# Grouping the narrow and wide matmul forms of a two-stage convolution, and storing the last two images in 8 KB pieces

## What is computed

```python
def _L0_conv_ref(x, w3, b3, w5, b5, wr, br):
    y3 = conv(x, w3, 'SAME') + b3
    y5 = conv(x, w5, 'SAME') + b5
    P = pad(y3, 1)
    shifts = [P[:, :, 2 - sw:2 - sw + H, 2 - sh:2 - sh + W] for sh in range(3) for sw in range(3)]
    stacked = stack([y5] + shifts, axis=2)
    return einsum('bcghw,cg->bchw', stacked, wr) + br

def _L1_conv_ref(x, filters):            # 3 x 3 patches, a leading 1, and all products of two entries
    spot = concatenate([ones, patches(x, 3)], -1)          # 10 numbers
    feat = spot[..., :, None] * spot[..., None, :]         # 100 products
    return einsum('bcyxf,ocf->boyx', feat, filters)

x = x + _L0_conv_ref(_gn(x), ...)
x = x + _L1_conv_ref(_gn(x), filters)
```

## Time and profile before

| | |
|---|---|
| median of 3 runs | 304.58 us |
| profiled execution, its own time | 305.6 us |
| its span | 303.9 us |
| mean granted TensorE clock | 0.979 |
| PE busy | 276.0 us (91%), 6464 records |
| DVE busy | 251.5 us (83%) |
| ACT busy | 88.1 us (29%) |
| DMA | 11.45 MB, of it 4.19 MB written |

### The profile page before, as it was taken

The page is one execution under the profiler, slowest core; times in us unless marked ns, Lnnn a source line. Parts: engine busy times, 40 slices in busy tenths (PEclk is TensorE's granted clock), DMA queues, the critical chain, the costliest instruction groups (busy, mean ns, idle before and its releaser), DMA issues.

```text
span 303.9 us, 13566 instructions
## 1 busy us (share of the span) xinstructions
PE 276.0 (91%) x6464; PEld 125.6 (41%) x6464; DVE 251.5 (83%) x216; ACT 88.1 (29%) x135; POOL 33.0 (11%) x82
## 2 busy tenths in 40 slices
PE   0579999899999999999999999999999999999930
PEld 0124443343334434436457455333334446447310
DVE  1899899995999999599999999976999999950330
ACT  5432016949258989529000000004000000000000
POOL 7913970000110000000000000000000000000000
PEclk9999999979999999999999999999999999999985
DMA  6973000000000000000000000085000000000049
GB/s 191 382 193 82 4 3 2 2 5 2 2 2 4 4 2 2 4 2 5 2 2 4 4 2 4 2 172 111 2 2 4 2 2 4 2 4 4 2 86 190
DMA packets 19206, 11.45 MB, mean 38 GB/s; under 512 B 17744, under 2 KB 17872, under 8 KB 19024
## 3 DMA queue, kind: packets, MB, share of 16 engines
q1 hardware_dynamic: 14640, 9.06, 11.7%
q10 hardware_dynamic: 4512, 1.53, 2.2%
HBM read 6.40 MB, written 4.19 MB: 35 GB/s over the span
## 4 chain that ended last, share of the span: by engine, by line
PE 80%; DVE 7%; ACT 3%; issue 3%; DMA 2%; SPq 1%; DVEq 0%
PE acc L1007 63%; PE acc L1050 15%; ACT raw L507 3%; DMA raw<-in_x 2%; DVE stats L741 2%; PE acc L1101 2%; DVE plane L759 1%; DVE raw L801 1%; DVE arena L669 1%; ACT arena L497 1%; DVE scaled L637 0%; DVE norm L756 0%; SPq L314 0%; SPq L321 0%; DVE mean_var L746 0%
## 5 line engine op out<-in xcount | busy, mean ns | idle before, releaser
L1007 PE MATMUL acc<-product,weight 32*32 32x512 f32 (+1 forms) x3040 | 128.6, 605 | 0.0
L1007 PEld LDWEIGHTS acc<-product,weight 32*32 32x32 f32 (+1 forms) x3040 | 61.7, 110 | 63.8 <-issue 51.1
L879 DVE TENSOR_TENSOR product<-plane 128x4096 f32<-128x4096 f32 x19 | 83.3, 4427 | 0.1
L1007 PE MATMUL acc<-raw,weight 32*32 32x512 f32 (+1 forms) x992 | 44.3, 605 | 0.0
L1050 PE MATMUL acc<-product,middle 32*64 32x512 f32 (+1 forms) x576 | 30.6, 621 | 0.0
L1007 PEld LDWEIGHTS acc<-raw,weight 32*32 32x32 f32 (+1 forms) x992 | 20.4, 111 | 20.7 <-issue 16.2
L801 DVE TENSOR_TENSOR raw<-acc,arena 128x512 f32<-128x512 f32 x16 | 9.9, 684 | 18.9 <-issue 18.7
L741 DVE BATCH_NORM_STATS2 stats<-raw 128x6 f32<-128x512 f32 x32 | 19.7, 686 | 3.1 <-DMA raw<-in_x 3.1
L879 DVE TENSOR_TENSOR raw<-plane 128x4096 f32<-128x4096 f32 x5 | 22.2, 4433 | 0.0
L1007 PE MATMUL acc<-product,arena 32*32 32x512 f32 (+1 forms) x448 | 22.0, 606 | 0.0
L507 ACT ACTIVATE raw<-arena 32x512 f32<-32x512 f32 x32 | 21.9, 683 | 0.5
(11 more groups left out here) (121 smaller groups left out, 213.9 us busy)
## 6 DMA issues: line engine op xcount, KB each, us to landing
raw<-in_x SPq DMA_DIRECT2D x8, 512.0 KB, 8.5
out<-raw SPq DMA_DIRECT2D x24, 128.0 KB, 2.9
arena<-in_L_conv_filters SPq DMA_DIRECT2D x4, 400.0 KB, 6.9
out<-raw ACTq DMA_DIRECT2D x8, 128.0 KB, 4.6
arena<-in_L_conv_w ACTq DMA_DIRECT2D x4, 100.0 KB, 4.0
w_in<-in_L_conv_w ACTq DMA_DIRECT2D x2, 36.0 KB, 1.9
w_in<-in_L_conv_w SPq DMA_DIRECT2D x2, 36.0 KB, 2.1
b_in<-in_L_conv_b SPq DMA_DIRECT2D x2, 0.5 KB
```

The lines of the kernel that those rows point to most:

```text
L879: nc.vector.tensor_tensor(both_halves(g, u), plane_halves(g), plane_halves(g, PRODUCTS[k][0] * PITCH + PRODUCTS[k][1]), ALU.mult)\
L1007: return nc.tensor.matmul(acc[32 * s:32 * (s + strips), j, r, :], weights[32 * r:32 * r + 32, t:t + strips, :] .rearrange("p t c -> p (t c ...
```

## The change

It has five parts.

1. In the second layer's mixed and side units the forms of several units are grouped: all pairs of linear, square and next one after another, then all singles, where before each unit had its own pair and single part. `mixed_unit` and `side_unit` now issue one form per call.
2. In `PRODUCTS` the entries (2, -1) and (1, -2) change places. The first is all singles, so that now (2, -1) and (2, 0) follow one another (units 15 and 16).
3. In the first layer of group 1 the border correction stands elsewhere: between its two parts there are 16 pairs of the block "total" instead of 16 singles, and the rest of that block starts with singles. In the second layer of group 0 the first 32 singles come ahead of the border's first part and the 32 pairs between its parts, where it was the other way round.
4. The last eviction (`evict_last`): images 0 and 1 as before. Images 2 and 3 are evicted strip by strip, 32 partitions x 512 elements each, straight into image layout on partitions 64 to 95 and 96 to 127 of `product[2]`.
5. Their store: SyncE and ScalarE's queue each send one half of the image rows of each of the two images, 256 KB, from 32 partitions, in runs of 8 KB. The small stores of images 0 and 1 stay.

```diff
-PRODUCTS = ((0, 0), (0, 1), (1, 1), (1, -1), (0, 2), (2, 2), (2, -2), (2, 1), (1, 2), (2, -1), (1, -2), (2, 0), (1, 0))
+PRODUCTS = ((0, 0), (0, 1), (1, 1), (1, -1), (0, 2), (2, 2), (2, -2), (2, 1), (1, 2), (1, -2), (2, -1), (2, 0), (1, 0))
...
+        def whole_image(r):
+            return product[2][32 * r:32 * r + 32, 0:PIX].rearrange("p (y x) -> p y x", x=W)
+
+        def store_last(eng, strips):
+            before = 2 * GROUP + 2 + 2 * STRIPS
+            for r in (0, 1):
+                eng.wait_ge(evicted, before + r + 1)
+                store(eng, 1, r, strips)
+            side = strips[0] // 2
+            for r in (2, 3):
+                eng.wait_ge(evicted, before + 2 + STRIPS * (r - 2) + 2 * side + 2)
+                eng.dma_start(out[GROUP + r][:, SIDE_ROWS * side:SIDE_ROWS * (side + 1), :],
+                              whole_image(r)[:, SIDE_ROWS * side:SIDE_ROWS * (side + 1), :]).then_inc(stored, 16)
...
+            def evict_last(odd):
...
+                for r in (0, 1):
+                    nc.vector.tensor_tensor(view(result, 2 * CHUNK * r + odd, (W, CHUNK // HALF_W), (2, HALF_W)),
...
+                for r in (2, 3):
+                    for s in range(STRIPS):
+                        y = SIDE_ROWS * (s // 2) + 1 - s % 2
+                        nc.vector.tensor_tensor(whole_image(r)[:, y:y + SIDE_ROWS - 1:2, odd:odd + W - 1:2],
+                                                acc[32 * s:32 * s + 32, odd, r, :]
...
+                                                ALU.add).then_inc(evicted, 1)
...
             product0(1, "next", 0, False, False, False)
             edges0(0, ROW_SIDES)
-            product0(1, "total", 0, False, False, False)
+            product0(1, "total", 0, False, False, True, (-1, 0))
             edges0(0, COLUMN_SIDES)
-            product0(1, "total", 0, False, True, True).then_inc(part_done, 1)
+            product0(1, "total", 0, False, False, True, (1, 2))
+            product0(1, "total", 0, False, True, False).then_inc(part_done, 1)
             pe.wait_ge(edges_copied, 2)
-            rest0(1, PAIRS_FIRST)
+            rest0(1, SINGLES_FIRST)
```

More of the change, by code:

```diff
@@ L604, in _ @@
             keep_cross(1)
-            for r in range(GROUP):
-                act.wait_ge(evicted, 3 * GROUP + r + 1)
-                store(act, 1, r, (2, 3))
+            store_last(act, (2, 3))
         @block.vector
@@ L1042, in plane_pixels, with column0 @@
                 return pixels
-            def column0(odd, stack, at, pitch, x0, every, five, start, stop, pairs):
+            def column0(odd, stack, at, pitch, x0, every, five, start, stop, pairs, rows):
                 def tile(r, s, strips, d, t, first_one, last_one):
@@ L1054, in column0 @@
                 if pairs:
[L1055 removed]
+                    for d in rows:
                         for s in (0, 2):
@@ L1064, in column0, with product0 @@
                 return last
-            def product0(g, name, odd, start, stop, pairs):
+            def product0(g, name, odd, start, stop, pairs, rows=range(-1, 3)):
                 if name == "next":
@@ L1070, in product0 @@
                     return column0(odd, plane[g], PLANE_AT - 2 * PITCH, PITCH, 2, 2, weight0[:, PAIR_AT:EDGE_AT, :],
-                                   start, stop, pairs)
+                                   start, stop, pairs, rows)
                 source, x0 = ("step", 1) if name == "step after" else (name, 0)
@@ L1077, in product0 @@
                 pe.wait_ge(middle_ready, g + 1)
-                return column0(odd, *half_at(g, source), x0, 1, five, start, stop, pairs)
+                return column0(odd, *half_at(g, source), x0, 1, five, start, stop, pairs, rows)
             def part(g, names, odd, forms):
@@ L1169, in mixed_unit, with side_unit @@
                     taps = (cross_taps if j else sum_taps)[0][:, 3:6, :]
-                for pairs in forms:
-                    last = column(j, stream_pixels(g, UNIT_OF[name][0], j), every_row, taps,
-                                  start and pairs == forms[0], stop and pairs == forms[-1], pairs)
-                return last
-            def side_unit(g, j, name, forms, start=False):
+                return column(j, stream_pixels(g, UNIT_OF[name][0], j), every_row, taps, start, stop, pairs)
+            def side_unit(g, j, name, pairs, start=False):
                 pe.wait_ge(stream_made, made(g, name + (" right" if j else " left")))
@@ L1181, in side_unit @@
                     a = {"linear": 0, "square": 9}[name] + 6 * j
-                for pairs in forms:
-                    last = column(j, stream_pixels(g, UNIT_OF[name][1], j), every_row, weight1[:, a:a + 3, :],
-                                  start and pairs == forms[0], False, pairs)
-                return last
+                return column(j, stream_pixels(g, UNIT_OF[name][1], j), every_row, weight1[:, a:a + 3, :],
+                              start, False, pairs)
             def taps1(g, j, u, pairs, stop=False):
```

96 lines of the change are left out of this document (62 added, 34 removed).

## The result

The changed kernel takes 303.59 us, the median of nine runs (302.55 to 304.27), beside 304.66 for nine runs of the kernel before. The ratio is 0.9945 (95% interval 0.9923 to 0.9967). The medians are 1.1 us apart, the ratio says 1.7 (1.0 to 2.3); 3.3 were forecast. The forecast of 301.3 was 2.3 us too low, though the time is inside its range. The profiled execution took 303.59 us too, with a span of 301.9.

A forecast was written before the change was run, and what follows sets the result against it. TensorE's pace and a store tail of some 10 us were taken as the bound. Runs -2.4, waits 0, first border -0.5, tail -0.1 and second border -0.3 made -3.3, from 304.58 to 301.3 us; range 298.4 to 303.9.

The forecast's parts named there:

- ten evictions 0.60 us apart: VectorE's last evictions: ten per half take 6.0 us, so half 1 starts at most 0.1 us late.
- The tail's rate: Final stores: large pieces from 32 partitions go at the filter load's rate, 219 GB/s at full share.
- The gain of 0.2: Final stores: 1 MB of large pieces takes 4.8 us against 5.0, with 0.1 us lost to the late start.
- the slower rival: Final stores: large pieces starve each other at half the filter's rate, tail 4.6 us longer, 306.0 us; chance 0.08.
- The rival at 408 GB/s: Final stores: large pieces run at the image load's rate, 2.3 us more off the tail, 299.0 us; chance 0.15.
- The runs of one form: TensorE behind 101 us: seven fewer changes from singles to pairs at 0.34 us each, 2.4 us less.
- the waits: TensorE, second layer: some 0.5 us more for square left, evened by the 0.6 us border-copy wait going; sum 0.
- The second border: Second layer's border correction, where 32 pairs now cover its start: estimated at 0.3 us less.
- The first border: First layer's border correction: stop shrinks from 1.8 to about 0.9 us, step done 0.35 us sooner; 0.5 us less in all.
- The clock: TensorE behind the first border: rival that the fall to 1.2 GHz goes too, worth 1.5 to 1.7 us, 299.7 us; chance 0.25.
- long waits for product streams: TensorE: rival that grouping turns into waits for streams, or the stop does not move, 303.7 us; chance 0.12.

The follow-up runs named there:

- e1: The changed kernel with the last evictions and stores of the kernel before: 302.1 us, ratio 0.9925 to the kernel before.
- e2: The kernel before with only the small evictions of images 2 and 3 and their stores in 8 KB runs: 305.9 us, ratio 1.0036.
- e7: The changed kernel with images 1 and 3 as the large stores, SyncE's queue sending all of image 1, ScalarE's all of image 3: 302.15 us, ratio 0.9903.
- e8: The changed kernel with the old tail and, in group 0, the singles of next ahead of those of square left: 302.71 us, ratio 0.993.
- e4: The kernel before with grouped forms, exchanged products and the second border's new order, but the old first border and tail: 303.41 us, ratio 0.9956.
- e5: The changed kernel with images 2 and 3 evicted in 32-partition pieces that stay in place, stored as before in small runs: 303.67 us, ratio 0.9968.

## Why the prediction was right in direction and wrong in size

**The failed step: ten evictions 0.60 us apart.** The prediction wrote that 32 partitions cost the same, that "ten take 10 x 0.60 = 6.0 us", and that half 1 starts at most 0.1 us late. The length was right (0.69 us either way), the distance was not. The overlap of 0.09 us that the large ones have was taken for granted, and it is lost wherever the starting partition changes: 2 x 0.60 + 0.12 + 8 x 0.72 = 7.1 us, and half 1 is 1.13 us late. Since half 1's stores are the tail, all of that is in the time: e1 against the changed kernel 1.1 us in the trace, e2 against before 1.1 us in the median. The number that was multiplied by ten came from the earlier trace rows, from evictions over 128 partitions; no row of before showed another shape at this place. The late start was put at 0.1 us and is 1.13; this alone takes 1.0 us of the 3.3 that were forecast. A bound was to be had: the page of before gives that line a mean length of 684 ns, so without overlap ten take 2 x 0.60 + 8 x 0.69 = 6.7 us at least.

**The tail's rate was as forecast.** The large pieces go at what the small ones did, 209 GB/s, and the tail stays 12.5 us. It had been taken from the filter load, 219 at full share, because the pieces are read from few partitions, and e7 supports that reason. The gain of 0.2 didn't come; the slower rival's half rate didn't either. The rival at 408 GB/s could not come in this form, with both queues on one half; e7 shows that 1.4 us of it were to be had.

**The runs of one form, -2.4, and the waits, 0.** The cost of a change was well sized: from the first pairs behind the second border (102.06 us before, 100.63 after) to half 0's first eviction there are 183.40 us before and 181.65 after, 1.75 less, and 2.35 without the wait that follows. One place stands out. Weight loads of the changed kernel, twice a run of 96 singles and the pairs behind it:

```profile
106.09 0.29 PEld L1039 LDWEIGHTS acc<-product,arena 32*32 32x32 f32 x32 [0.81 <-DVE product L911]
...
109.90 0.24 PEld L1039 LDWEIGHTS acc<-product,weight 32*32 32x32 f32 x32 [1.24 <-DVE product L904]
...
113.33 0.23 PEld L1039 LDWEIGHTS acc<-raw,weight 32*64 32x64 f32 x16 [0.89 <-issue]
...
143.69 0.29 PEld L1039 LDWEIGHTS acc<-product,weight 32*32 32x32 f32 x32 [0.85 <-issue]
...
150.33 0.23 PEld L1039 LDWEIGHTS acc<-raw,weight 32*64 32x64 f32 x16 [0.88 <-issue]
```

The first run takes 113.33 - 106.09 = 7.24 us, the second 150.33 - 143.69 = 6.64: 0.60 us are the wait for "square left". The prediction had named it, at 0.5, and set against it the wait for ScalarE's border copy, 0.6. That one did not go: it is 0.5 still. So the term of the waits is +0.5, not 0: the second step that failed. The prediction set one wait off against another that it only supposed to end. (e8 shows that without it TensorE would meet most of it again further down.)

**The second border, -0.3.** TensorE's timeline from the second layer's start to the first mixed single behind its border, first of the kernel before, then of the changed one:

```profile
91.44 4.01 PE L1007 MATMUL acc<-plane,arena 32*64 32x512 f32 x64 [0.69 <-DVE arena L669]
...
100.65 0.67 PE L1007 MATMUL acc<-product,arena 32*32 32x512 f32 x6
```

```profile
90.34 2.52 PE L1039 MATMUL acc<-plane,arena 32*32 32x512 f32 x64 [0.74 <-DVE arena L681]
...
99.23 0.58 PE L1039 MATMUL acc<-product,arena 32*32 32x512 f32 x1
```

100.65 - 91.44 = 9.21 us have become 99.23 - 90.34 = 8.89, so 0.3 less, as forecast. The second layer as a whole went from 194.02 to 191.94 us, 2.1 less, where -2.4 - 0.3 + 0.5 = -2.2 is the corrected sum. In the other traces with grouped forms it lies between 191.7 and 192.6, and in those without between 194.0 and 194.1, so 1.4 to 2.4 us less, which takes in the 1.6 us of the medians.

**The first border, -0.5.** Right in its trace (the stop is gone, or shrunk to 0.2 to 0.5), and 0.4 to 0.8 by the medians. One part of its sum is off: the last 32 pairs behind the border were taken at 3.49 us, without what a run costs, where the earlier trace rows has 3.69, so that "step" should have come 0.14 us sooner and not 0.35. A single trace can't tell it: the border's first part waits for VectorE, whose work up to there comes from the image's load, and starts at 57.47 in e2 and 58.23 in the changed kernel, though nothing ahead of it was changed. What the stop gives is smaller than that spread.

**The clock.** The rival had it worth 1.5 to 1.7 us. Of the 90 runs of before nine have a mean granted clock of 0.979 or less, the others 0.983 or more, and the mean time of the nine is 306.4, 1.5 above the median of all. With the border moved none of 95 runs has 0.979 or less. Seven of these are at 0.981 or 0.982, where the mean can't decide, since it also moves with the stretch at 1.2 GHz behind TensorE's end, which is 9.1 to 12.5 us long in the traces. The traces decide better. Of the four with the old order two show the fall, before and e4, and they are the ones with the longest stops of all, 1.54 and 1.17 us; the ten with the border moved show none. So the fall goes with the long stop, as the rival said, but it was in about one run of ten. It moves the mean by 0.15 us and the median by nothing. The prediction had left it out of the sum; its chance of 0.25 hung on a question that the three times of before, 1.0 us under the profiled one, had half answered.

Together: -2.2 (second layer), -0.4 to -0.8 (first border), +1.1 (tail) make -1.5 to -1.9, with the second layer taken from the traces. With the 1.6 us of the medians in its place they make -0.9 to -1.3. The ratio says -1.7, the medians -1.1. Of the 3.3 us that were forecast 1.2 were lost at the end (+1.1 where -0.1 stood) and 0.5 in the wait. That the time still lies inside the range is in part luck: its high end was set for another rival, long waits for product streams, which didn't come.

## What to carry to other kernels

A pace read from evictions that all start at the same partition does not hold for pieces that start at different ones: read length and distance of starts apart, and bound the new pace by the length. Idle time of an engine that is filled to its last tenth needs that bound, because every excess moves to the end. When two queues store large pieces at once, read them from partition ranges 64 apart; long runs alone, from one half, brought nothing here. Where an engine stops for nothing that the profile shows, look whether instructions were being loaded.

## What the runs showed of the hardware

- VectorE adding PSUM and SBUF in fp32, 512 elements: 0.69 us in length over 128 and over 32 partitions. Starts are 0.60 us apart where both read and write from the same starting partitions (over 128, and once in each half of e5 over 32), and 0.68 to 0.73 where the starting partition changes.
- Runs of 8 KB from partitions 64 to 127 by both queues move 209 GB/s, no more than runs of 256 bytes that were spread over both halves. With one queue on each half the tail's second part goes at 229 GB/s with the DMA engines less busy (0.84 instead of 0.93), and an 8 KB packet takes 344 ns in the median instead of 628.
- TensorE's stop between the border parts differs from run to run: 0.80 to 1.54 us in the four traces with the old order, 0 to 0.52 in the ten with the new one. It stands at the same instruction in each, and where it is over 0.6 us between two starts it ends 1.3 to 1.5 us after a 16 KB packet of the instruction queue has landed.
- The fall of TensorE's clock right behind the border is just as uneven. A mean clock of 0.979 or less marks it only roughly: e4's profiled execution has a mean of 0.982 and still shows the fall in its window from 63.0 to 66.4:

```profile
63.00:66.40 3.40, 3.40 (x40) 1.28 (x32) 3.32 (x5) 2.34 (x8) 0.00 (x0) 0.50 0.02 5
```
